# Two cross attentions on one core: projections cut into halves and dealt out anew, and the seam's query projection moved ahead of its keys

## What is computed

```
x = x + tanh(g_xattn[0]) * xattn0(layernorm(x), ctx, ctx)   # 16 heads of width 32
x = x + tanh(g_ffn[0])   * ffn0(layernorm(x))               # 512 -> 2048, conv of 3, silu, -> 512
x = x + tanh(g_xattn[1]) * xattn1(layernorm(x), ctx, mask)  # 8 heads of width 64, masked
x = x + tanh(g_ffn[1])   * ffn1(layernorm(x))               # gate, up, down in rounded fp4

q, k, v = x @ Wq, ctx @ Wk, ctx @ Wv          # by heads
attn = softmax(q @ k.T * scale)               # [.. 224, 750]
out  = (attn @ v) @ Wo
```

## Time and profile before

| | us |
|---|---|
| median of 3 runs | 2287.61 (2285.31 to 2291.52) |
| the profiled execution | 2280.43 |
| its span, first to last instruction | 2278.6 |

### The profile page before, as it was taken

The page is one execution under the profiler, slowest core; times in us unless marked ns, Lnnn a source line. Parts: engine busy times, 40 slices in busy tenths (PEclk is TensorE's granted clock), DMA queues, the critical chain, the costliest instruction groups (busy, mean ns, idle before and its releaser), DMA issues. The chain is left out here.

```text
span 2278.6 us, 42253 instructions
## 1 busy us (share of the span) xinstructions
PE 1975.2 (87%) x15208; PEld 1385.9 (61%) x15208; DVE 1477.8 (65%) x2752; ACT 949.6 (42%) x1289; POOL 1214.7 (53%) x1470
## 2 busy tenths in 40 slices
PE   5798898898897478989588898998999977899997
PEld 3466666666666367778355676666666664455553
DVE  4766666666656479897454556655656546898973
ACT  3266666666657573333133334334333443111111
POOL 4166666657756453333221556566666422777763
PEclk9899999999999589999788999999999988899998
DMA  7354344344331231111253443434444422011100
GB/s 208 94 123 107 92 108 118 94 112 119 96 92 41 99 97 33 40 32 33 86 162 93 114 124 116 135 118 136 123 127 132 127 83 65 28 33 33 36 23 28
DMA packets 184011, 208.67 MB, mean 92 GB/s; under 512 B 61480, under 2 KB 145704, under 8 KB 183336
## 3 DMA queue, kind: packets, MB, share of 16 engines
q1 hardware_dynamic: 183848, 206.46, 32.0%
HBM read 138.61 MB, written 67.53 MB: 90 GB/s over the span
## 5 line engine op out<-in xcount | busy, mean ns | idle before, releaser
L678 POOL TENSOR_TENSOR a_p_hl<-a_p,a_p_hl 125x448 bf16<-125x448 f32 x540 | 578.7, 1073 | 533.8 <-ACT a_p_hl L811 505.3
L811 ACT ACTIVATE a_p_hl<-a_p 125x1344 bf16<-125x1344 f32 x192 | 254.0, 1323 | 140.4 <-PE a_psum L1227 137.4
L801 ACT ACTIVATE a_p<-a_psum 125x1344 f32<-125x1344 f32 x192 | 247.7, 1290 | 130.5 <-PE a_psum L1189 123.0
L977 DVE TENSOR_REDUCE a_nm<-a_psum 112x1 f32<-112x750 f32 x256 | 236.4, 930 | 24.9 <-PE a_psum L1209 23.0
L1227 PEld LDWEIGHTS a_psum<-a_v_st,a_p_hl 125*128 125x128 bf16 x4608 | 185.4, 100 | 39.7 <-issue 19.7
L1227 PE MATMUL a_psum<-a_v_st,a_p_hl 125*128 125x65 bf16 (+2 forms) x4608 | 196.7, 198 | 9.5 <-ACT a_p_hl L811 3.1
L1209 PE MATMUL a_psum<-a_k_st,a_q_st 96*112 96x375 bf16 x512 | 134.0, 348 | 77.5 <-DVE a_nm L977 72.4
L1856 PE MATMUL f_conv<-f_u,f_taps 128*128 128x224 f32 x768 | 161.6, 360 | 22.2 <-DVE f_u L1708 21.3
L942 DVE TENSOR_TENSOR a_v_st<-a_psum,a_v_st 125x512 bf16<-125x512 f32 x96 | 66.4, 691 | 171.9 <-ACT a_v_st L779 171.9
L1117 PE MATMUL a_psum<-a_chl,kept_w 128*128 128x375 bf16 x768 | 141.9, 339 | 24.4 <-DVE kept_w L868 18.3
L1856 PEld LDWEIGHTS f_conv<-f_u,f_taps 128*128 128x128 f32 x768 | 141.9, 192 | 31.7 <-DVE f_u L1708 27.0
(11 more groups left out here) (251 smaller groups left out, 4045.5 us busy)
## 6 DMA issues: line engine op xcount, KB each, us to landing
a_k<-a_k_tmp SPq DMA_DIRECT2D x64, 375.0 KB, 2.9
a_k_st<-a_k SPq DMA_DIRECT2D x96, 187.5 KB, 3.4
kept_k<-a_k SPq DMA_DIRECT2D x96, 187.5 KB, 3.4
a_c<-in_ctx_t SPq DMA_DIRECT2D x16, 750.0 KB, 5.8
ctx_parts<-a_chl SPq DMA_DIRECT2D x16, 750.0 KB, 9.2
a_chl<-ctx_parts SPq DMA_DIRECT2D x16, 750.0 KB, 6.7
a_q_st<-a_q SPq DMA_DIRECT2D x192, 56.0 KB, 2.2
rounded<-a_fw SPq DMA_DIRECT2D x24, 352.0 KB, 3.7
```

The costliest lines, as they stand in the source:

```text
L678: ins = nc.gpsimd.tensor_tensor(p_hl[0:MC, h % 2, 1, cols], p32[0:MC, h % 2, cols], p_hl[0:MC, h % 2, 0, cols], ALU.subtract)
L801: nc.scalar.activation(p32[0:MC, par, :].rearrange("p (b n) -> p b n", b=3), st[0:MC, :, 0:2 * S], ACT.Exp, scale=scale).then_inc(exp_done, 1)
L811: nc.scalar.activation(p_hl[0:MC, par, 0, :], p32[0:MC, par, :], ACT.Copy).then_inc(phi_done, 1)
L977: ins = nc.vector.tensor_reduce(out, sm_[0:HALF, 0:2, 0:MK], AX.XY, ALU.max, negate=True)
```

## The change

**First attention.** A table `PLACES` gives each unit a first and a last place among a quarter's 16. Where they differ (four K units and all V but V1 and V3, and both OP: ten of a row), TensorE issues the first six of its 12 matmuls at the first place and the other six at the last; ScalarE and VectorE treat the unit at the last. The units are dealt out anew: V3 goes from q = 1 to q = 0, K (1, 0) and Q 1 of a row go from q = 0 to the q = 3 before, X 0 goes from q = 3 to q = 2, M 1 from the start of q = 0 to its third head, and in q = 3 K (0, 1) now comes ahead of Q 0. On VectorE the low part of a unit at slot 4j + 2 comes behind the second `maximum` of the head, no longer ahead of it. The chunks of the context split and the normalising come one half head earlier, and ScalarE splits the second context half behind X 0 in q = 2 instead of behind K (0, 0) in q = 3. OP 0 waits for the unit two before it (OT 1, since Q 2 stands between) and Q 0 too.

**Second attention.** In q = 3 the order X0, X1, K (0, 0), K (0, 1), Q 0 at slots 0, 1, 3, 4, 6 becomes X0, X1, Q 0, K (0, 0), K (0, 1) at slots 0, 0, 2, 3, 4. SyncE loads context half 0 behind the regroup of Q 3. The weight piece that was loaded behind Q 0 in q = 3 is loaded in the next q = 0, where K (1, 0) stands.

```diff
     def quarter_units(q, b):
+        if stacked:
+            row, far = b + 1, b + 2
+            units = (
+                [("K", (1, 1), row), ("V", 0, row), ("V", 1, row), ("M", 1, b), ("V", 2, row), ("V", 3, row)],
+                [("K", (2, 0), row), ("OT", 0, b + -1), ("K", (2, 1), row), ("OT", 1, b + -1), ("Q", 2, row),
+                 ("OP", 0, b + -1), ("OP", 1, b + -1)],
+                [("K", (3, 0), row), ("K", (3, 1), row), ("Q", 3, row), ("M", 0, row), ("V", 4, row), ("V", 5, row),
+                 ("X", 0, far)],
+                [("K", (0, 0), far), ("X", 1, far), ("K", (0, 1), far), ("Q", 0, far), ("K", (1, 0), far),
+                 ("Q", 1, far)])[q]
+            return [u for u in units if u[2].exists() and not (u[:2] == ("M", 1) and b.number == 0)]
...
-            if stacked and q == 3 and chunk:
-                units = chunk[:1] + units + [chunk[2], chunk[1]]
+            if q == 3:
+                units += chunk[2:] + chunk[:2]
...
+    PLACES = (
+        {("K", (1, 1)): (0, 2), ("V", 0): (4, 6), ("V", 1): (8, 8), ("M", 1): (10, 10), ("V", 2): (10, 12),
+         ("V", 3): (14, 14)},
+        {("K", (2, 0)): (0, 0), ("OT", 0): (2, 2), ("K", (2, 1)): (2, 4), ("OT", 1): (6, 6), ("Q", 2): (6, 6),
+         ("OP", 0): (8, 10), ("OP", 1): (12, 14)},
+        {("K", (3, 0)): (0, 0), ("K", (3, 1)): (2, 2), ("Q", 3): (4, 4), ("M", 0): (6, 6), ("V", 4): (6, 8),
+         ("V", 5): (10, 12), ("X", 0): (14, 14)},
+        {("K", (0, 0)): (0, 2), ("X", 1): (4, 4), ("K", (0, 1)): (6, 6), ("Q", 0): (8, 8), ("K", (1, 0)): (10, 12),
+         ("Q", 1): (14, 14)})
...
-        if stacked and q == 3 and units:
-            at = [1, 2, 4, 6, 9]
+        if q == 3 and units:
+            at = [0, 0, 2, 3, 4]
...
-                      12: [("Q", 0, nb)]}
+                      12: [("Q", 0, nb)], 13: [("K", (1, 0), nb)], 14: [("Q", 1, nb)]}
...
+                if q == 0:
+                    if unit == ("K", (1, 0), b + 1) and 2 <= m < FP4_PIECES:
+                        sp.wait_ge(fw_sent, (m - 1) * 16)
+                        load_weight_piece(m)
-                if unit[0] == "Q" and 1 <= m < FP4_PIECES - 1:
+                if unit[0] == "Q" and q != 3 and 1 <= m < FP4_PIECES - 1:
...
-                        if unit[:2] == ("K", (KC - 1, 1)):
+                        if unit[:2] == ("Q", KC - 1):
                             load_ctx(b + 2, 0)
...
-                    if stacked and unit[:2] == ("K", (0, 0)) and (b + 2).exists():
+                    if stacked and q == 2 and unit[:2] == ("X", 0):
                         split_ctx(b + 2, 1, None)
...
-                    for unit in slots[4 * j + 2]:
-                        unit_step(unit)
+                    if not stacked:
+                        for unit in slots[4 * j + 2]:
+                            unit_step(unit)
...
                         maximum(b + 1, h, 1)
+                    if stacked:
+                        for unit in slots[4 * j + 2]:
+                            unit_step(unit)
...
-            CHUNKS = {(2, 3): [(0, 0), (0, 1)], (2, 4): [(0, 2), (0, 3)],
-                      (3, 1): [(1, 0), (1, 1)], (3, 2): [(1, 2), (1, 3)]}
+            CHUNKS = {(2, 2): [(0, 0), (0, 1)], (2, 3): [(0, 2), (0, 3)],
+                      (3, 0): [(1, 0), (1, 1)], (3, 1): [(1, 2), (1, 3)]}
-            NORMALISED = {(2, 5): [0], (2, 7): [1]} if stacked else {(2, 2): [0], (2, 3): [1]}
+            NORMALISED = {(2, 4): [0], (2, 6): [1]} if stacked else {(2, 2): [0], (2, 3): [1]}
...
-                for c in range(KC):
+                for c in {"whole": range(KC), "first": range(KC // 2), "second": range(KC // 2, KC)}[part]:
...
+            def place_products(q, b, slot):
+                for unit in quarter_units(q, b):
+                    first, last = PLACES[q][unit[:2]]
+                    if slot == last:
+                        unit_products(unit, "whole" if first == last else "second")
+                    elif slot == first:
+                        unit_products(unit, "first")
...
-                if kind == "OP" and k == 0 or unit[:2] == ("Q", 0) and stacked and (b.number is None or b.number >= 2):
+                if (unit[:2] == ("OP", 0) and not (stacked and (b + 2).exists())
+                        or unit[:2] == ("Q", 0) and not stacked and (b.number is None or b.number >= 2)):
                     pe.wait_ge(unit_done, n - 1)
```

More of the change, by code:

```diff
@@ L1119, in project, with unit_products @@
                 return ins
-            def unit_products(unit):
+            def place_products(q, b, slot):
[5 more added lines that the diff above has]
+                        unit_products(unit, "first")
+            def unit_products(unit, part="whole"):
                 kind, k, b = unit
+                if part == "second":
+                    unit_matmuls(unit, units.bank(), part).then_inc(unit_mm, 1)
+                    return
                 n = units.next()
-                bank = units.bank()
                 if kind in ("K", "V"):
```

44 lines of the change are left out of this document (28 added, 16 removed).

## The result

| | before | after |
|---|---|---|
| median, us | 2286.46 (2279.32 to 2291.52, 4 runs) | 2224.74 (2223.13 to 2231.33, 4 runs) |
| the profiled execution | 2280.43 | 2225.15 |
| its span | 2278.6 | 2223.4 |

In the traces the second attention starts 22.9 us earlier (its first K unit at 1119.1 instead of 1142.0 us), and the last matmul of its output projections starts 55.3 us earlier (at 1821.6 instead of 1876.9); that is the whole difference of the two profiled executions, so behind it nothing changes. So the first attention gave 23 us and the second 32 us.

What follows compares the result with a forecast made beforehand. TensorE was taken as the bound, losing time in short waits. Six rows at 2.1 and 4.1 us saved gave 13 + 25 = 38 us off 2280.4, 2242 us; with 7.2 us for the median, 2249 us, range 2206 to 2281.

Steps and rivals of the forecast that it cites:

- (a): First attention, q = 2: VectorE's work comes in a lump, so TensorE waits for maxima, 2.2 us a row.
- (b): First attention: the second context half arrives late, 3.0 us a row on TensorE, 1.3 at scores and 1.6 at K (0, 1).
- (c): First attention's seam: with Q 0 written behind K (0, 1), TensorE waits 2.8 us a row, where it was 1.26.
- (d): First attention, third head of q = 1: OP 0 waits for OT 1's low part on VectorE, 1.8 us.
- (e): Second attention's seam: Q 0 goes ahead and K (0, 1) is last; the wait falls from 4.1 to 1.0 us.
- (f): Second attention: Q 3's write no longer stands behind a context load, so its wait, 0.9 us mean, goes.
- (g): Second attention: X 1 directly behind X 0 waits for VectorE to normalise the second half, a new 1.6 us.
- (h): Second attention: both context halves are loaded together and later; K (0, 1) waits 0 to 3 us, taken as 1.0.
- rival 1: Halves pay in full in the first attention, rows under 84 us; 2206 us with the second's gain; 15%.
- Rival 4: Slower: more, smaller waits in both attentions each pull TensorE's clock down; 2316 us with five of seven; 7%.
- Rival 2: The first attention gains nothing, as (b) and (c) at 4.5 us each eat the gain; 2262 us; 15%.
- rival 3: The second attention gains nothing: (g) and (h) at 3 us, clock falling in the same places; 2275 us; 12%.

Runs made afterwards that it cites:

- e2: The kernel before with the second attention's edits alone; 2246.23 us, ratio 0.9854 to the kernel before.
- e10: The kernel before with 16 useless matmuls ahead of the first scores of rows 2 to 7 in the second attention; 2280.64 us, ratio 0.9958.
- after_again: The changed kernel itself, timed and traced once more; 2231.16 us, ratio 0.9750 to the kernel before.
- e1: The changed kernel with all edits of the second attention undone; 2256.42 us, ratio 0.9910 to the kernel before.
- e3: The changed kernel with X 1 of the second attention back at slot 1, behind the transposed scores; 2211.69 us, ratio 0.9712 to the kernel before.
- e12: The changed kernel with the second attention's context half 0 loaded behind K (3, 1) again; 2232.97 us, ratio 0.9750 to the kernel before.
- e7: The changed kernel with Q 0 ahead of K (0, 1) in q = 3 of the first attention; 2227.70 us, ratio 0.9737 to the kernel before.
- e8: The e7 kernel with the last two context chunks moved behind the first maximum of head 13; 2220.01 us, ratio 0.9707 to the kernel before.
- e6: The changed kernel with VectorE's low part ahead of the head's second maximum again in the first attention; 2227.34 us, ratio 0.9729 to the kernel before.

## Why the prediction was right, and where it was short

The direction held, and most of the waits stood where the walk put them. The sum was short: 2242 us for the profiled execution, which took 2225.15, so by 17 us. The other 7 us of the 24 are the 7.2 us that were added because the median of the runs before lay that far above the profiled execution; after the change the two agree (2224.74 and 2225.15). By its own steps:

- **(a) Maxima**: 2.2 us a row forecast for the lump of q = 2, 12.2 / 6 = 2.0 measured for all maxima. In the trace half of it stands at the end of q = 2 and half in the first two heads of q = 3, of which the walk of q = 2 did not speak, so that the numbers agree is partly luck.
- **(b) The second context half**: ScalarE was to wait 1.5 us, and waited 8.9 us in six rows, 1.5. Of the price on TensorE the part at K (0, 1) was 1.6, and was 1.9; but 0.9 of that is the pair of chunks that takes 1.94 us instead of 1.00, which the walk did not have, so the term came out by luck. The 1.3 us at the scores hardly came, 1.5 us in two waits, 0.25 a row. 3.0 became 2.2.
- **(c) The seam**: 2.8 forecast (its terms give 2.9), 16.6 / 6 = 2.8 measured. The queue's path was as described: keys first, then the write of the queries, 4.8 us (431.50 to 436.29).
- **(d) OP 0**: 1.8 forecast, 1.5 measured.
- **Waits of the first attention, mis-sized**: they were to rise from 9.0 to 9.8 us a row. By the table idle time fell from 46.4 (mean of before, e2, e10) to 41.6 us (after, after_again, e1, e3, e12) in five rows, from 9.3 to 8.3 a row. So the forecast was 1.8 us a row short here: 0.8 in (b), 0.3 in (d), 0.2 in (a), 0.3 in the waits of before; the rest is not located.
- **Pipeline ends and clock of the first attention**: the forecast had the ends fall from 2.4 us to nothing and the clock's loss from 3.1 to 2.6, together 2.9 us a row of busy time. Busy time fell by 2.8. That is luck too, for the clock's loss fell further than forecast, from a mean of 19.9 to 10.9 us in five rows (4.0 to 2.2 a row), and at least 1.0 of the 2.8 is left for the ends, where 2.4 was put. The price of before was too low because it was taken from one stretch around 442 us; in the trace of before the clock falls at that place in four rows of five, and some 10 us further on in three. The loss also has the largest spread: 8.5 and 17.1 us in two executions of one kernel.
- **(e) The seam of the second**: 1.0 forecast, 5.2 / 6 = 0.9 measured. From X 0 to the seam's scores are 22.0 us (1343.13 to 1365.16); 22 to 23 was forecast.
- **(f) Q 3's wait** went, but for 0.9 us in six rows. That the context load held up Q 3's write is shown by e12 (medians of 7.1 against 3.5 us); but X 1's wait would have covered it too.
- **(g) X 1**: 1.6 forecast, 1.4 measured, and e3 gave it back whole.
- **(h) The pair of context loads, mis-sized**: 1.0 us a row was put on it and none came. The longest landing was 7.5 us from a load's issue, and TensorE waited for neither half in any row, so the case in which the second load begins only when the first has landed (13 us behind X 0) did not occur. The Trainium skill (DMA: Bandwidth & Descriptors, Queues, rings and completion order) has each DMA engine consume its descriptors in ring order. The small write that took 7.4 instead of 4.8 us behind a load agrees with that; what failed is my reading that the second load then starts when the first has landed.
- **(i)** Nothing, as forecast: no wait of TensorE leads to the weight pieces.
- **Clock and ends of the second**: 2.3 us a row forecast (1.8 and 0.5). Busy time fell from 412.9 (before, e1) to 402.7 us (after, after_again, e2), 2.0 a row. e10 supports the clock's share: 1.3 us of busy time a row come back when the seam alone is filled.
- **Waits of the second, mis-sized**: 1.8 a row less forecast, (29.0 - 11.5) / 5 = 3.5 measured. 1.0 of the difference is (h), 0.3 is (e) and (g), and 0.4 are small waits of before that I didn't count (its idle time is 5.8 a row by e1 and before, 5.4 were put down to queries).

The rows: 2.1 and 4.1 us forecast, 3.7 and 5.5 measured. 3.0 us a row on the forecast's six rows are 18 us, which is the 17 us that the sum was short. The waits alone are 1.8 and 1.7 us a row of it; busy time, clock and ends together, came out 0.1 and 0.3 below the forecast. So it was the waits that the forecast had too dear, (b) and (h) above all, and not the clock.

The rivals: rival 1 asked for rows under 84 us in the first attention; they last 84.7 to 86.2, so it falls by its own sign, although the median lies nearer to its 2206 us (19 us) than to the forecast's 2249 (24 us). Rival 4, slower by the clock, had the sign wrong. In the second attention the waits that stayed cost the clock little: 0 to 5.1 us were lost in five rows in the eleven traces that have the changed second attention, and 15.4 and 17.1 in before and e1. In the first its picture does not fit: idle time was not in one or two lumps before but in 71 waits for maxima, and is now in fewer and longer ones, up to 3.7 us. There the clock falls at two of them, at K (0, 1)'s wait and at the seam's, as (b) and (c) had it. Rival 2, nothing gained in the first attention, is excluded by e1, rival 3, nothing in the second, by e2, and rival 5 by the result.

Left open is why one execution of the changed kernel loses twice as much to the clock in the first attention as another with the same waits. In the first trace it falls at K (0, 1)'s wait in one row of five and at the seam in four, in after_again in four and in three.

## What to carry to other kernels

Waits that other engines impose can be walked with durations from the trace: five of seven came within 0.3 us, the other two ((b) and (h)) were 0.8 and 1.0 us too dear. Where a bound engine waits in a lump, add what the clock loses behind it: taking most of a wait of 4 us away gave back 2 us of busy time a row on top of the wait itself. Take that price from several rows and executions, not from one stretch. A wait that is taken away often comes back one step down the same chain (e7 to e8, e6), so follow the last queue to its end, here the write behind the queries' reads, before counting the gain. And units cut in half, with one half at each side of a dependency, fed the engine through it, where the same order with whole units did not.

## What the runs showed of the hardware

- Useless matmuls in a wait made the kernel faster: 3.4 us of filling in each seam, 0.42% off the whole (e10, interval 0.25 to 0.59%).
- The time lost to the clock differed between two executions of one program by 8.6 us in five rows, with idle times of 41.4 and 41.3 us.
- Two context loads of 750 KB issued back to back landed in 4.8 to 7.5 us, median 5.6; apart, they took 4.9 to 7.6 us, median 6.6, in steady rows of before.
- A small write of 112 KB behind such a load took some 3.5 us longer until what follows it could be issued (medians of six rows: 7.1 us in e12, 3.5 in the changed kernel).
- A pair of context chunks on VectorE took 1.94 us in one place of every row of the changed kernel, and 1.00 us in the kernel before; in e6 and e8, where the order around it differs, it took 1.00 us. Why is open.
